# A plan column of the expert stage made 32 bits wide and masked, and one early tile in place of three

## The chip, the cores and the metric

The kernel runs on one core of one Trainium2 chip. The metric is the device time of one execution in microseconds (us). Five engines work side by side, each with an instruction queue of its own: TensorE (PE, matrix products; its weight loads are shown apart as PEld), VectorE (DVE), ScalarE (ACT), GpSimd (POOL) and SyncE (SP), which here only issues transfers (DMA). A name with a q behind it (PEldq, ACTq, SPq) is what the engine's own sequencer does without the engine: loads of registers, sums in registers, issues of transfers. Engines wait for each other through counting semaphores.

## What is computed

4096 tokens of width 256 (64 sequences of 64) go through a conditioned adapter, one attention layer and a mixture of 32 experts, of which each token takes four:

```python
x = adapter(x, cond)                              # down, relu, up, residual
x = x + attention(rmsnorm(x)) @ proj_w            # 16 heads, 64 keys, sinks
h2 = rmsnorm(x)
topv, topi = top_k(h2 @ gate_w + gate_b, 4)
gw = softmax(topv)
for each expert e:                                # W_up 256x512, W_down 256x256
    u, g = split(h2 @ W_up[e])
    y += combine[:, e] * (silu(g) * u @ W_down[e])
out = x_in + x + y
```

Only the experts that a token chose count: 4096 tokens by 4 choices are 16384 pairs of a token and an expert.

## The kernel before

**Two parts.** The first part (adapter, attention, router) ends by writing the chosen rows into lists in memory, one list for each expert (`put`, L673, POOL). The second part, which the change touches, takes the lists in tiles of 128 rows. All values are float32; products are split in two parts, so that an expert's up-product is six matmuls of 512 columns (L971) and its down-product six of 256 (L990).

**The tiles.** How full each list is is known only at run time. The number of tile steps is therefore a fixed upper bound, `NET = PAIRS // P + E - 1 + (AHEAD - 1)`. With `AHEAD = 3` that is 161. For these inputs 142 tiles hold rows; the steps behind them do the same work on rows that go nowhere. The first tiles of the first `AHEAD` experts are at places known beforehand (`begun_slot`, `load_rows` with `i < AHEAD`), and all others come from a plan.

**The plan.** When the router is done, DVE works out the plan (L1559 to L1629) as rows of 256 entries on one partition: `plan_slot` (the offset of the tile's weights in a ring of four experts in SBUF), `plan_wait` (how many experts' weights must have arrived, 1 to 32) and `plan_list` (where the tile's rows lie). The engines read the plan into registers, eight tiles at a time (`BATCH = 8`): PE `plan_slot` (L952) and `plan_wait` (L958), ACT `plan_list` (L1240). `plan_wait` is a tile of type uint16, the other two are int32.

**The loop on PE** (from L1002) does this in step i: the second turn of tile i-2 (`turn_mid`, L980), the first turn of tile i+2 (`turn_in`, L945: two transposes, and the second waits for `s_wready` to reach the register from `plan_wait`), the up-product of tile i (`expert_up`), in every eighth step a read of the plan (`load_slots` at i % 8 == 5, `load_readies` at i % 8 == 6), and the down-product of tile i-3 (`expert_down`).

**Around it.** ACT issues the load of a tile's rows six steps ahead (`load_rows`, L1251), splits, applies silu and scales the result (`rows_out`, L1233). POOL scatters the result rows (L695). SP loads weights (L567) and, once all tiles with rows are through and six more counts of `s_rows_out` have come (`all_out`), starts to read the scattered rows back: eight transfers `picks` of 2 MB (L609) into five buffers; the sixth, seventh and eighth wait until DVE and PE have used a buffer.

**The end.** Behind its last tile, DVE adds up eight groups of picked rows (L1685, L1687, L1690), with no wait but for the picks; PE and ACT add a quarter of each group beside it, the first of them after all scatters have landed; SP and ACT store the result.

Of the kernel before, what the change touches and what calls it, by code (L numbers as in the profile page):

```python
# [8 lines left out]

F32, I32, U32, BF16 = mybir.dt.float32, mybir.dt.int32, mybir.dt.uint32, mybir.dt.bfloat16  # L10
U16 = mybir.dt.uint16
F32R = mybir.dt.float32r
ACT = mybir.ActivationFunctionType
AX = mybir.AxisListType
# [2 lines left out]
P = 128  # L17
# [22 lines left out]
ROW = D + LINE  # L40

PAIRS = NTOK * TOPK
AHEAD = 3
NET = PAIRS // P + E - 1 + (AHEAD - 1)
NET2 = 4 * -(-(NET - P) // 4)
RING = 4
# [18 lines left out]
BATCH = 8  # L65
# [155 lines left out]
def program(nc, d):  # L221
# [4 lines left out]
    def sb(name, shape, dt=F32, stack=ctx):  # L226
        return stack.enter_context(nc.sbuf_tensor(name, shape, dt))
# [19 lines left out]
    expert_no = sb("expert_no", [P, E])  # L247
    begun_slot = sb("begun_slot", [1, AHEAD], I32)

# [115 lines left out]
    plan_f = sb("plan_f", [1, 2 * P])  # L365
    plan_e = sb("plan_e", [1, 2 * P], I32)
    plan_slot = sb("plan_slot", [1, 2 * P], I32)
    plan_wait = sb("plan_wait", [1, 2 * P], U16)
    ring_wait = sb("ring_wait", [1, E], I32)
    all_out = sb("all_out", [1, 1], I32)  # L370
    rows_in = [sb(f"rows_in{i}", [P, ROW]) for i in range(NG)]
# [92 lines left out]
    EARLY, MIDDLE, LATE = 16 * len(early), 16 * len(middle), 16 * len(late)  # L464
    FILL, BEFORE = 16 * (AHEAD + 1), 16 * E
    LAST = NT - 1
# [13 lines left out]
    def sync_program(e):  # L480
# [52 lines left out]
        def load_late():  # L533
            for dst, src in late:
                e.dma_start(dst, src).then_inc(s_late, 16)

            for at in [n * LIST + P for n in range(AHEAD)] + [E * LIST]:
                e.dma_start(lists[at:at + P, :], d["fill_rows"]).then_inc(s_fill, 16)
# [166 lines left out]
    def tensor_program(e):  # L705
# [219 lines left out]
        for h in range(2):  # L925
# [6 lines left out]
        _, at = nc.values_load_multi_w_load_instructions(  # L932
            begun_slot[0:1, 0:AHEAD], engines=[mybir.EngineType.PE], min_val=0, max_val=(RING - 1) * 2 * WE,
            skip_runtime_bounds_check_because="the table holds ring offsets")
        slot_of = {i: (at[i], i + 1) for i in range(AHEAD)}

# [12 lines left out]
        slots, readies = {}, {}  # L949
# [11 lines left out]

        def slot(i):
            if i >= AHEAD:
                slot_of[i] = (slots[i // BATCH][i % BATCH], readies[i // BATCH][i % BATCH])
            return slot_of[i]

        def expert_up(i):
# [34 lines left out]
        for i in range(NET + 3):  # L1002
            if i == 5:
                w.wait_ge(s_plan_list, 1)
            if 2 <= i < NET + 2:
                turn_mid(i - 2)
            if i < NET:
                ready = slot(i)[1]
                if 0 < i < NET - 2:
                    turn_in(i + 2, ready)  # L1010
                else:
                    e.wait_ge(s_wready, ready)
                expert_up(i)
                if i == 0:
                    turn_in(2)

            if i % BATCH == BATCH - 3 and i + 3 < NET:
                load_slots(i // BATCH + 1)
            if i % BATCH == BATCH - 2 and i + 2 < NET:
                load_readies(i // BATCH + 1)  # L1020
            if i >= 3:
                expert_down(i - 3)
# [775 lines left out]
```

## Time and profile before

| | |
|---|---|
| median of 3 runs | 1040.16 us (1039.16 to 1040.64) |
| the profiled execution | 1039.19 us |
| its span, first to last instruction | 1037.4 us |
| the expert stage, from the first tile's up-product to DVE's last tile | 583.1 to 1002.4 us |
| the end, DVE's eight groups and the last store | 1002.4 to 1037.4 us |
| PE busy over the span | 895.6 us (86%) |

The page gives one execution. Read it in three stretches: the first part up to about 556 us, the change-over (plan, last scatters into the lists, first tiles) to about 593 us, and the tiles and the end behind that. The share of PE is a mean over all of them. In the tiles PE goes without a gap, in the change-over it mostly waits. How a stretch ends is read from the chain of work that ended last, and who waited for whom from the idle time that the timeline puts in brackets behind a row.

### The profile page before, as it was taken

The numbers are of one execution on the slowest core, as the hardware profiler recorded it, in microseconds if no ns is written. First come the engines' busy times: TensorE is split into PE (matmuls) and PEld (weight loads), VectorE is DVE, ScalarE is ACT, GpSimd is POOL, SyncE is SP. The second block draws the span as 40 slices with busy tenths as digits, with TensorE's granted clock in tenths as the row PEclk, the third lists the DMA queues.
The fourth block names the chain that finished last, engine by engine and source line by source line (L and its number), as shares of the span: only waits on it lengthen the run. The fifth ranks groups of instructions, "written<-read, shape, count | busy, mean of one in ns | idle before, by whom it ended". The sixth has DMA issues, their size and how long they took to land.

```text
span 1037.4 us, 21388 instructions
## 1 busy us (share of the span) xinstructions
PE 895.6 (86%) x7240; PEld 728.6 (70%) x7272; DVE 804.4 (78%) x1877; ACT 512.5 (49%) x1193; POOL 550.4 (53%) x513
## 2 busy tenths in 40 slices
PE   3859898997899989888851599999999999999985
PEld 2537676675676767567640488888888888888864
DVE  3878799898888889887755377777777777777777
ACT  1223463736445363553751366665665666566631
POOL 2436557877868687887778034333333333333440
PEclk8769999999899999999995699999999999999998
DMA  7235869687796977869875977778677758663589
GB/s 223 61 95 179 267 234 269 212 286 245 243 283 206 291 249 253 271 224 292 306 246 206 336 261 270 277 237 282 238 239 263 257 184 306 227 219 103 189 334 349
DMA packets 127683, 251.93 MB, mean 243 GB/s; under 512 B 18706, under 2 KB 66327, under 8 KB 127002
## 3 DMA queue, kind: packets, MB, share of 16 engines
q1 hardware_dynamic: 83866, 187.59, 54.8%
q0 software_dynamic: 13872, 34.64, 9.2%
q10 hardware_dynamic: 29840, 28.34, 8.8%
q8 instruction: 62, 1.02, 0.4%
q14 instruction: 43, 0.35, 0.1%
HBM read 136.19 MB, written 102.66 MB: 230 GB/s over the span
## 4 chain that ended last, share of the span: by engine, by line
PE 49%; POOL 12%; DMA 12%; DVE 11%; issue 7%; ACT 4%; SPq 4%; ACTq 0%; DVEq 0%; POOLq 0%
PE gbank L971 10%; PE scores L971 10%; POOL lists L673 7%; PE gbank L990 5%; PE scores L990 5%; DMA w_parts<-ring 4%; DMA ring<-in_W_up 3%; PE gbank L762 3%; DMA rows_in<-lists 3%; POOL ring L680 3%; PE gbank L843 3%; PE scores L945 2%; DVE ring L1402 2%; PE gbank L980 2%; PE gbank L945 2%
## 5 line engine op out<-in xcount | busy, mean ns | idle before, releaser
L695 POOL DMA_INDIRECT pick_rows<-rows_out,pair_i x161 | 160.7, 998 | 277.3 <-ACT rows_out L1233 268.5
L680 POOL TENSOR_TENSOR ring<-ring 128x512 fp32r<-128x512 f32 x96 | 123.2, 1296 | 47.3 <-ACT ring L1168 46.6
L971 PE MATMUL scores<-ring,in_part 128*128 x486 | 135.9, 415 | 0.0
L971 PE MATMUL gbank<-ring,in_part 128*128 x480 | 131.8, 409 | 0.0
L673 POOL DMA_INDIRECT lists<-put_rows,slot_i x104 | 101.5, 976 | 49.9 <-issue 27.3
L762 PE MATMUL gbank<-h_t,w_qk 128*128 128x512 f32 x480 | 122.0, 407 | 7.0 <-DVE h_t L1389 4.7
L843 PE MATMUL gbank<-w_o,ring 128*128 128x256 f32 x512 | 118.3, 385 | 3.8 <-ACT ring L1114 3.7
L1402 DVE SCALAR_TENSOR_TENSOR ring<-gbank,b_qk,rope 128x512 f32<-128x512 f32 x160 | 109.9, 744 | 14.7 <-PE gbank L762 14.1
L762 PEld LDWEIGHTS gbank<-h_t,w_qk 128*128 128x128 f32 x480 | 89.6, 191 | 32.2 <-issue 8.6
L843 PEld LDWEIGHTS gbank<-w_o,ring 128*128 128x128 f32 x512 | 96.2, 193 | 17.3 <-ACT ring L1114 5.2
L1168 ACT ACTIVATE ring<-ring 128x512 fp32r<-128x512 f32 x96 | 59.9, 628 | 92.2 <-DMA w_parts<-ring 49.1
L971 PEld LDWEIGHTS scores<-ring,in_part 128*128 128x128 f32 x486 | 86.9, 192 | 15.2
L971 PEld LDWEIGHTS gbank<-ring,in_part 128*128 128x128 f32 x480 | 84.3, 189 | 14.5
L990 PEld LDWEIGHTS gbank<-ring,mid_part 128*128 128x128 f32 x486 | 67.1, 188 | 14.6 <-issue 8.1
L1219 ACT ACTIVATE in_part<-scores,norm_w 128x128 fp32r<-128x128 f32 x162 | 50.8, 365 | 51.8 <-PE scores L945 33.4
L990 PE MATMUL gbank<-ring,mid_part 128*128 x486 | 70.3, 280 | 4.2 <-issue 4.1
L990 PEld LDWEIGHTS scores<-ring,mid_part 128*128 128x128 f32 x480 | 66.8, 188 | 7.2
L990 PE MATMUL scores<-ring,mid_part 128*128 x480 | 68.2, 278 | 0.0
L1649 DVE SCALAR_TENSOR_TENSOR mid<-scores,rows_in,silu 128x256 f32<-128x256 f32 x81 | 39.1, 483 | 36.7 <-ACT silu L1225 36.7
L1225 ACT ACTIVATE silu<-scores,rows_in 128x256 f32<-128x256 f32 x81 | 38.6, 477 | 52.0 <-PE scores L971 51.9
L1639 DVE TENSOR_TENSOR pair_i<-rows_in,twice 128x1 int32<-128x1 f32 x161 | 25.7, 160 | 49.0 <-ACT in_part L1219 40.0
L1649 DVE SCALAR_TENSOR_TENSOR mid<-gbank,rows_in,silu 128x256 f32<-128x256 f32 x80 | 38.5, 482 | 27.1 <-ACT silu L1225 27.1
(200 smaller groups left out, 1879.2 us busy)
## 6 DMA issues: line engine op xcount, KB each, us to landing
w_parts<-ring SPq DMA_DIRECT2D x192, 256.0 KB, 3.3
ring<-w_parts SPq DMA_DIRECT2D x32, 1536.0 KB, 7.6
rows_in<-lists ACTq DMA_DIRECT2D x161, 136.0 KB, 4.0
ring<-in_W_up SPq DMA_DIRECT2D x64, 256.0 KB, 3.5
picks<-pick_rows SPq DMA_DIRECT2D x8, 2048.0 KB, 11.9
ring<-in_W_down SPq DMA_DIRECT2D x32, 256.0 KB, 4.0
q_r<-rot SPq DMA_DIRECT2D x16, 512.0 KB, 6.8
q_r<-ring SPq DMA_DIRECT2D x16, 512.0 KB, 6.5
```

The costliest lines, as they stand in the source:

```text
L673: e.indirect_dma_start(out=lists, out_offset=bass.IndirectOffsetOnAxis(ap=slot_i[r % NPAY][:, s * TOPK + k:s * TOPK + k + 1], axis=0), in_ ...
L680: e.tensor_tensor(lower, lower.bitcast(F32), upper.bitcast(F32), ALU.subtract).then_inc(s_lower, 1)
L695: e.indirect_dma_start(out=pick_rows, out_offset=bass.IndirectOffsetOnAxis(ap=pair_i[:, i:i + 1], axis=0), in_=rows_out[i % NY][:, :], in_ ...
L762: ins = e.matmul(bank[:, :], w_qk[:, x, c, 2 * j + o, :], h_t[i][:, y, c, :], start=k == 0, stop=k == len(CHUNK_PRODUCTS) - 1)
L843: ins = e.matmul(bank[:, 0:D], y_t[:, n // REP, n % REP, :, :].rearrange("p b s -> p (b s)"), w_o[:, n, :], start=False, stop=n == 2 * REP ...
L945: ins = e.transpose(bank[:, c * P:(c + 1) * P], rows_in[i % NG][:, c * P:(c + 1) * P], ident[:, :])
L971: ins = e.matmul(front[i % FRONTS], in_parts[i % IN_BUFS][x][:, c, :], ring[:, bass.ds(at + y * WE + c * 2 * DFF, 2 * DFF)], start=k == 0, ...
L990: ins = e.matmul(out, mid_parts[i % 2][x][:, c, :], ring[:, bass.ds(at + y * WE + KC * 2 * DFF + c * D, D)], start=k == 0, stop=k == len(C ...
L1168: e.activation(w_upper[q % NU], w_third[q % NW].bitcast(F32), ACT.Copy).then_inc(s_upper, 1)
L1219: ins = e.activation(in_parts[i % IN_BUFS][0][:, c, :], front[i % FRONTS][:, c * P:(c + 1) * P], ACT.Copy, scale=norm2_w[:, c:c + 1])
L1402: e.scalar_tensor_tensor(out=by_seq(t[n][:, :]), in0=by_seq(gbank[banks[o]][:, :]), scalar=b_qk[:, 2 * j + o:2 * j + o + 1], in1=rope[:, t ...
L1649: e.scalar_tensor_tensor(out=mid[i % MID_BUFS][:, :], in0=front[i % FRONTS][:, 0:DFF], scalar=rows_in[i % NG][:, D + 2:D + 3], in1=silu[i ...
```

## The change

Three things are edited. `AHEAD` goes from 3 to 1: only the first tile of the first expert is begun without the plan, the second and third tile come from the plan as well, the bound `NET` falls from 161 to 159, and with it the steps of PE, DVE, ACT and POOL; `begun_slot`, the rows of `list_begin` and `tile_no` and the number of lists that are filled beforehand follow. `plan_wait` becomes int32. And the value that `turn_in` waits for is masked with 63 in a register. The tiles that hold rows are 142 as before.

```diff
-U16 = mybir.dt.uint16
...
-AHEAD = 3
+AHEAD = 1
 NET = PAIRS // P + E - 1 + (AHEAD - 1)
...
-    plan_wait = sb("plan_wait", [1, 2 * P], U16)
+    plan_wait = sb("plan_wait", [1, 2 * P], I32)
...
             if i >= AHEAD:
-                slot_of[i] = (slots[i // BATCH][i % BATCH], readies[i // BATCH][i % BATCH])
+                slot_of[i] = (slots[i // BATCH][i % BATCH], readies[i // BATCH][i % BATCH] & 63)
             return slot_of[i]
```

On PE, this is the step in which `plan_wait` is read for the second time (i = 6), before the change: the second turn of one tile and the first turn of another (both transposes in one row, x2), the up-product, the read.

```order
478 L980 MATMUL gbank<-ident,mid 128x128 x2
479 L945 MATMUL scores<-ident,rows_in 128x128 x2
480 L971 ISA
481 L971 MATMUL gbank<-ring,in_part 128x512
482 L971 ISA
483 L971 MATMUL gbank<-ring,in_part 128x512 x2
484 L971 ISA
485 L971 MATMUL gbank<-ring,in_part 128x512
486 L971 ISA
487 L971 MATMUL gbank<-ring,in_part 128x512 x2
488 L958 TENSOR_LOAD plan_wait
489 L990 ISA
```

The same step on PE after the change (line numbers are one lower, since a line of the file is gone; an ISA row is a sum in registers that makes an address):

```order
488 L979 MATMUL gbank<-ident,mid 128x128 x2
489 L944 MATMUL scores<-ident,rows_in 128x128
490 L943 REGISTER_ALU
491 L944 MATMUL scores<-ident,rows_in 128x128
492 L970 ISA
493 L970 MATMUL gbank<-ring,in_part 128x512
494 L970 ISA
495 L970 MATMUL gbank<-ring,in_part 128x512 x2
496 L970 ISA
497 L970 MATMUL gbank<-ring,in_part 128x512
498 L970 ISA
499 L970 MATMUL gbank<-ring,in_part 128x512 x2
500 L957 TENSOR_LOAD plan_wait
```

One register operation has come between the two transposes of `turn_in`, in this step and in every other one that takes its wait from the plan (158 tiles). Nothing else on PE moved; the 21st reads of `plan_slot` and `plan_wait`, for tile 160, are gone with the last two steps.

On ACT, this is the start of the row loads before the change, three of them ahead of the read of the plan:

```order
408 L1251 DMA rows_in<-lists 128x272 x3
409 L1240 TENSOR_LOAD plan_list
410 L1251 REGISTER_ALU
411 L1251 DMA rows_in<-lists 128x272
412 L1251 REGISTER_ALU
```

And after it:

```order
408 L1250 DMA rows_in<-lists 128x272
409 L1239 TENSOR_LOAD plan_list
410 L1250 REGISTER_ALU
411 L1250 DMA rows_in<-lists 128x272
412 L1250 REGISTER_ALU
413 L1250 DMA rows_in<-lists 128x272
```

The read of the plan has moved ahead of the loads of tiles 1 and 2, and each of these two takes a register operation of its own. DVE, POOL and SP keep their order; DVE and POOL do two tiles fewer at the end, and SP fills two lists fewer at the start of the program.

## Rows read from the trace of the kernel before

**Rows 1.** Timeline of PE: start, us, engine line; the up-products of tiles 8 and 48.
```profile
606.24 1.65 PE L971 MATMUL scores<-ring,in_part 128*128 x6
...
707.42 1.64 PE L971 MATMUL scores<-ring,in_part 128*128 x6
```

**Rows 2.** Lines L958, L952: ns min/median/max, first and last start; last row 605 to 710.
```profile
L958 PEldq TENSOR_LOAD <-plan_wait x21: 1923/2011/2420, 563.8 to 992.6; - x21
...
L952 PEldq TENSOR_LOAD <-plan_slot x21: 587/594/1532, 562.2 to 988.5; - x21
...
L958 PEldq TENSOR_LOAD <-plan_wait x5: 1927/1977/2042, 619.9 to 700.9; - x5
```

**Rows 3.** Line L958 from 743 to 746 us, and PE's timeline there (tile 62).
```profile
L958 PEldq TENSOR_LOAD <-plan_wait x1: 1923/1923/1923, 743.6 to 743.6; - x1
...
745.05 1.65 PE L971 MATMUL gbank<-ring,in_part 128*128 x6
```

**Rows 4.** The same around tile 54: weight loads and PE; idle time before in brackets.
```profile
723.29 0.20 PEld L945 LDWEIGHTS scores<-ident,rows_in 128*128 128x128 f32 x2 [0.38 <-DMA rows_in<-lists]
...
L958 PEldq TENSOR_LOAD <-plan_wait x1: 2072/2072/2072, 723.9 to 723.9; - x1
...
726.15 0.98 PE L990 MATMUL gbank<-ring,mid_part 128*128 x6 [1.02 <-issue]
```

**Rows 5.** PEld's waits, 593 to 988.9 us (total, times, longest); PE's timeline, tiles 3, 157.
```profile
PEld gbank L990 <- issue: 6.5, 8, 1.4
PEld scores L945 <- DMA rows_in<-lists: 1.1, 3, 0.5
...
593.02 1.18 PE L971 MATMUL gbank<-ring,in_part 128*128 x4
...
988.90 1.65 PE L971 MATMUL scores<-ring,in_part 128*128 x6
```

**Rows 6.** Register operations of L971 (PE) and L1251 (ACT); L945's transposes: busy, mean ns.
```profile
L971 PEldq FUSED_REGOPS  x644: 42/46/51, 582.9 to 996.7; - x161
...
L1251 ACTq ALU_OP  x158: 46/46/53, 575.8 to 984.3; - x158
...
L945 PE MATMUL gbank<-ident,rows_in 128*128 128x128 f32 x160 | 31.1, 277 | 1.1 <-DMA rows_in<-lists 1.1
```

**Rows 7.** The chain that ended last, 555 to 600 us: start, us, what.
```profile
569.60 3.84 DMA lists<-q_r,slot_i
...
575.07 0.74 ACTq L1240
...
575.99 11.49 DMA rows_in<-lists
...
587.52 0.69 PE gbank L945 x2
```

**Rows 8.** PE's timeline over the last tiles; first row and last from the chain.
```profile
984.41 7.57 DMA rows_in<-lists
...
992.22 1.65 PE L971 MATMUL gbank<-ring,in_part 128*128 x6
994.70 0.97 PE L990 MATMUL gbank<-ring,mid_part 128*128 x6 [0.82 <-issue]
...
995.64 1.65 PE L971 MATMUL gbank<-ring,in_part 128*128 x6
...
1002.37 1.68 DVE picks L1685
```

**Rows 9.** SP's timeline; stretches: busy by engine, PE clock, DMA share, GB/s; the chain's end.
```profile
974.07 44.50 SPq L609 DMA_DIRECT2D picks<-pick_rows  x8
...
1000.00:1005.00 5.00, 4.87 (x33) 4.30 (x32) 4.69 (x7) 2.03 (x5) 3.26 (x3) 1.00 0.78 299
1005.00:1010.00 5.00, 2.80 (x13) 2.11 (x12) 4.90 (x6) 0.00 (x0) 3.05 (x2) 1.00 0.56 177
...
1030.64 0.96 DVE resid L1690
```

## The prediction

> **What bounds the kernel now.** I read the timeline of PE over the tiles first, then the registers' reads, then the change-over and the end.
>
> In the tiles PE's array is the bound. The up-product of tile 8 starts at 606.24 us and that of tile 48 at 707.42 [rows 1]: 40 steps in 101.18 us, 2.53 us each. A step has no idle time of PE in it; what the array has to do more adds to the time, and what lies in PE's sequencer alone adds nothing as long as the sequencer is ahead of the array.
>
> That it is ahead can be seen. In these 101 us PE's sequencer read `plan_wait` five times, and each read held it for 1.93 to 2.04 us [rows 2]; the step stayed 2.53. At tile 62 the read starts at 743.6 although it is queued behind the up-product that the array begins only at 745.05 [rows 3]: a lead of 1.45 us, to which the 1.65 us of that up-product is added. A read of 1.92 us is over at 745.5, before the array runs dry.
>
> Where the lead is lost, the read shows. At tile 54 a late load of rows held PE for 0.38 us, the read began at 723.9, behind the start of its own tile's up-product (723.29 plus 0.20, 723.5), took 2.07 us, and the down-product began only at 726.15 with 1.02 us of idle time put down to "issue" [rows 4]. The waits of the weight loads list eight such places between 593 and 988.9 us, all of them in one form, the one behind `plan_wait` [rows 5]. `plan_slot`, as many entries of 32 bits, takes 0.594 us in the middle, against 2.011 [rows 2].
>
> In the change-over the chain runs through the last scatters into the lists, then ACT's load of tile 3, 11.49 us under way, then PE [rows 7]. At the end it runs through DVE's eight groups, 1002.37 to 1031.60 us without a gap [rows 8, 9], with the picks' transfers beside it.
>
> **The change part by part.** All sums are made against the profiled execution, 1039.19 us (span 1037.4).
>
> *The 32-bit read, 21 times, then 20.* From tile 3 (593.02) to tile 157 (988.90) there are 154 steps in 395.88 us [rows 5]. At 2.53 (101.18/40) they would take 389.54; 6.34 are stalls. 1.1 of it are three waits for rows [rows 5]; the other 5.2 are the eight reads. (The row's own 6.5 counts from the idle weight loader and is an upper end.) If the new read costs what `plan_slot` costs, the worst case of tile 54 reads: 723.9 plus 0.59 is 724.5, while the array is on the up-product until 723.5 plus 1.65, 725.1. Nothing is left. Gain 5.2; with the three waits for rows it could at most be 6.3. A read that is only a little shorter gains less; that is the first rival. The first read, before tile 0, is hidden by the wait for rows either way. DVE writes one row of 256 entries as 32 bits in place of 16, before the same wait.
>
> *Two steps fewer.* The 142 tiles with rows are the same in both kernels, so the picks start behind the same tile. What goes are two of the steps behind them: 2 times 2.53, 5.06 us, on PE, which is on the path until DVE's first group.
>
> *The last tiles' stalls.* From tile 157 to 158 the step is 3.32 (988.90 to 992.22), to 159 it is 3.42 [rows 5, 8]. The first is the wait for the last rows: their load was issued at 984.41, ten microseconds behind the first picks (974.07), and took 7.57 us [rows 8, 9]. The last load of the new kernel is issued two steps earlier behind the picks, so it still arrives in time. The second is the 21st read of `plan_wait`, which is gone [rows 8]. 0.79 and 0.89, together 1.7.
>
> *The register operation, 158 times.* The trace of before has none like it on PE. The nearest rows: 644 fused sums of registers on the same sequencer at 46 ns behind L971 alone, and ACT's single sum at 46 ns [rows 6]. Below end: 0, hidden by the lead. Upper end: 158 times 0.046, 7.3 us. I take 0, since in [rows 1, 2] the sequencer gets back 2.0 plus 0.6 us of reads in eight steps without a stall, at least 0.32 a step, which is seven times the new operation; and the reads then want 1.2 in place of 2.6.
>
> *The start.* Tile 0's rows are loaded as before. Tiles 1 and 2 now come behind the read of the plan (0.74 us [rows 7]); the plan is long there, since the loads wait for the last scatters. PE turns tile 3 before the second up-product, and tile 3's load has the same transfers and the same read ahead of it, plus two register operations and moves, about 0.1 each. Loss 0.25; upper end 1.0, if tile 1's late load binds. The weights of experts 1 and 2 are wanted later than before, which costs nothing.
>
> *The end.* DVE's groups start 5.06 plus 1.7, 6.8 us nearer to the first picks. Does the transfer hide that? Between 974.07 and the end the DMA engines are filled but for 1000 to 1010 us, where the shares are 0.78 and 0.56 [rows 9]: 5 times 0.22 plus 5 times 0.44, 3.3 us free. Two row loads of 136 KB less at about 0.3 MB a us give 0.9. If all of that traffic has to be moved, the end can come only 4.2 us nearer to the first picks, and 2.6 are given back. If the later transfers, which wait for buffers, have slack, nothing is. The first five are under way at once, so they land before they are wanted; the sixth to eighth wait for buffers and stay close to DVE. I take the middle, 1.3.
>
> Sum: 5.2 + 5.06 + 1.7 - 0.25 - 1.3 = 10.4 us, 1028.8 for an execution like the profiled one. That one is at the low end of the three runs, 0.97 below their median; I add half of it: **1029.3 us**.
>
> **The rivals.**
>
> *The read stays long.* The column is read at another place than `plan_slot`; if it is the place or the time and not the 16 bits that makes 2.0 us, little is gained. With none of the 5.2 us won the time is 1034.5. For it: 2.011 us are 251 ns for each of eight registers, which looks like one trip after another. Against it: eight registers of 32 bits take 74 ns each, on the same engine, one step earlier [rows 2]. The Trainium skill (Runtime: NRT & Kernel Launch, Instruction fetch mechanics) puts a register's load at about 200 ns even in bulk; by that rule a read of eight would take 1.6 us whatever its width, an estimate, eight stalls would lose at most 8 times 0.41, 3.3 us, and the time would be 1031.2 or more. The trace disagrees with it for 32 bits and comes near it for 16.
>
> *The transfers bind the end.* The full 2.6 us are given back: 1030.6.
>
> *The register operation shows.* If the sequencer has no time to spare, 7.3 us come back (158 times 46 ns): 1036.6, still 0.3% faster. Against it stand the steps of 2.53 with two reads in every eight.
>
> *Slower.* The wait of the second transpose takes its value from a register that has just been written. If PE's sequencer ran the operation only when the first transpose has left the array, the lead would be gone in each tile, and a step would grow by up to one transpose, 277 ns [rows 6]: 158 times 0.277 is 43.8, that is 1029.3 + 43.8 = 1073.1 us. It decides from 66 ns a tile (10.4/158). Against it: the fused sums stand between matmuls too, and their products' addresses come from them at once, with no gap.
>
> **How the numbers follow.** The forecast 0.73; the transfers bind the end 0.12; the read stays long 0.05; the register operation shows 0.06; slower 0.04. Range: the best sum is 6.3 + 5.06 + 1.7 with nothing given back, 13.1, which is 1026.1; the worst within the forecast gives back 2.6 and loses 1.0 at the start, 8.4, which is 1030.8, or 1031.8 with the whole distance to the median; the first rival takes it to 1034.5. 1026 to 1034.5 leaves out the register cases and the tails, under 0.2. What this kernel's measurement can tell from no change is about 0.2%, 2.1 us: faster 0.92, within it 0.04 (the register operation together with the transfers, 1038), slower 0.04.
>
> **What the profile of the changed kernel would show.** The reads of `plan_wait` at about 0.6 us, 20 of them; no "issue" idle time ahead of L990 in the gbank form; steps of 2.53 throughout, so that tile 3 to tile 157 take about 390.6; the last L971 row followed by DVE's first group without a wait for rows; picks starting about 5 us earlier, DVE's first group about 12. A step of 2.57 to 2.58 would mean that the register operation shows; idle time ahead of L945's second transpose, that the lead is lost; a gap between DVE's groups or PE waiting for picks longer than now, that the transfers bind. The prediction is wrong if the reads are not shorter or the step grows.

## The result, and the profile after the change

The changed kernel takes **1031.08 us** (median; the kernel before, timed beside it, 1040.52), a ratio of **0.9914 with a 95% interval of 0.9889 to 0.9938**: between 6.5 and 11.5 us faster. The forecast was 1029.3 us in a range of 1026 to 1034.5, 10.9 us faster. A second comparison of the same two kernels gave 1034.03 against 1041.13, 0.9918 (0.9897 to 0.9939). (The ratios are taken over all the runs, not from the two medians.) The time lies in the range both times. The accounts below show that the size came out nearly right partly by terms that cancel.

The profiled execution of the changed kernel took 1029.53 us, its span is 1027.7 (before: 1039.19 and 1037.4). Its line numbers are one lower than those of before: L958 is now L957, L971 is L970, L990 is L989, L1685 is L1684.

The reads of the registers and the new operation, in the changed kernel (ns minimum/median/maximum, first and last start in us):

```profile
L957 PEldq TENSOR_LOAD <-plan_wait x20: 587/590/692, 563.7 to 965.9; - x20
...
L951 PEldq TENSOR_LOAD <-plan_slot x20: 587/592/1584, 562.0 to 963.3; - x20
...
L943 PEldq ALU_OP  x156: 32/32/42, 587.1 to 981.9; - x156
```

The read of `plan_wait` fell from a median of 2.011 us [rows 2] to 0.590, that is what `plan_slot` takes. The mask is there as a 32 ns operation of PE's sequencer, 156 times between two transposes. (The section on the change said 158: the other two masks belong to the last two steps, which have no first turn left, and stand ahead of the up-product.) The waits of the weight loads from 590 to 1000 us (total, times, longest), first in the kernel before, then in the changed one; [rows 5] has the stretch from 593 to 988.9 us alone:

```profile
PEld gbank L990 <- issue: 7.8, 9, 1.4
PEld scores L945 <- DMA rows_in<-lists: 1.9, 4, 0.8
```

```profile
PEld gbank L944 <- DMA rows_in<-lists: 1.9, 2, 1.2
PEld scores L944 <- DMA rows_in<-lists: 0.5, 1, 0.5
PEld scores L989 <- issue: 0.4, 1, 0.4
```

The "issue" time behind the reads is gone, 6.5 us between tiles 3 and 157 and 7.8 up to 1000 us; the one of 0.4 is in the other form. Waits for rows are 2.4 us, all of them between tile 3 and the fourth last, where they were 1.1 in that stretch. Now PE's timeline, the up-products of tiles 3, 32, 48, 155 and 158 (start, us):

```profile
590.94 1.40 PE L970 MATMUL gbank<-ring,in_part 128*128 x5
...
665.92 1.64 PE L970 MATMUL scores<-ring,in_part 128*128 x6
...
706.62 1.64 PE L970 MATMUL scores<-ring,in_part 128*128 x6
...
980.10 1.63 PE L970 MATMUL gbank<-ring,in_part 128*128 x6
...
987.28 1.64 PE L970 MATMUL gbank<-ring,in_part 128*128 x6
```

This is the surprise. From tile 32 to 48 the 16 steps take 40.70 us, **2.544 us each and not 2.53**. Nothing waits there; the step itself is longer. The products behind it, first in the kernel before, then in the changed one (640 to 960 us: busy us, mean ns of one, idle before):

```profile
L990 PE MATMUL gbank<-ring,mid_part 128*128 x372 | 53.6, 280 | 3.0 <-issue 3.0
L990 PE MATMUL scores<-ring,mid_part 128*128 x372 | 52.8, 277 | 0.0
```

```profile
L989 PE MATMUL gbank<-ring,mid_part 128*128 x378 | 55.2, 282 | 0.0
L989 PE MATMUL scores<-ring,mid_part 128*128 x375 | 54.8, 282 | 0.0
```

At the end, DVE's eight groups (first and last start) and, in the changed kernel, the one wait among them:

```profile
L1685 DVE TENSOR_TENSOR picks<-picks x8: 1748/1750/1753, 1002.3 to 1027.9; 128x1536 f32<-128x1536 f32 x8
```

```profile
L1684 DVE TENSOR_TENSOR picks<-picks x8: 1749/1751/1758, 991.6 to 1018.3; 128x1536 f32<-128x1536 f32 x8
...
  DMA picks<-pick_rows: 1.0, 1
```

The two profiles differ by 9.7 us of span. Put together from the starts of the up-products and of DVE's groups:

| stretch | before, us | after, us | difference |
|---|---|---|---|
| up to tile 0's up-product | 583.13 | 582.92 | -0.2 |
| tile 0 to tile 3 | 9.89 | 8.02 | -1.9 |
| tile 3 to the fourth last tile (157, now 155) | 395.88 | 389.16 | -6.7 |
| from there to DVE's first group | 13.4 | 11.5 | -1.9 |
| DVE's first group to its last | 25.6 | 26.7 | +1.1 |
| from there to the end | 9.5 | 9.4 | -0.1 |

The -6.7 of the third row are four things: two steps fewer, -5.06; 152 steps that are each 13.9 ns longer (means of the undisturbed steps 2.5432 and 2.5293), +2.1; the reads' stalls gone, -5.26; and 1.5 us more of waiting for rows.

### The profile page after: what moved, and what is told of

The parts are those of the page before. It is cut to its first block, busy times and chain, and to the rows that moved or that the text cites. A ratio compares the mean times of both kernels' runs of the same rounds, so it can differ in the third digit from the quotient of the medians.

```text
span 1027.7 us, 21467 instructions
## 1 busy us (share of the span) xinstructions
PE 891.4 (87%) x7240; PEld 727.2 (71%) x7240; DVE 802.3 (78%) x1865; ACT 509.0 (50%) x1185; POOL 549.9 (54%) x511
## 4 chain that ended last, share of the span: by engine, by line
PE 48%; POOL 14%; DMA 13%; DVE 9%; issue 8%; SPq 5%; ACT 3%; ACTq 0%; POOLq 0%; DVEq 0%
PE scores L970 10%; PE gbank L970 10%; POOL lists L672 9%; PE scores L989 5%; PE gbank L989 5%; DMA w_parts<-ring 4%; PE gbank L761 4%; DMA rows_in<-lists 3%; DMA ring<-in_W_up 3%; POOL ring L679 3%; PE gbank L842 3%; PE gbank L944 2%; DVE ring L1401 2%; PE gbank L979 2%; PE scores L944 2%
## 5 line engine op out<-in xcount | busy, mean ns | idle before, releaser
L970 PE MATMUL scores<-ring,in_part 128*128 x480 | 132.2, 411 | 0.0
L970 PE MATMUL gbank<-ring,in_part 128*128 x474 | 129.3, 408 | 0.0
L970 PEld LDWEIGHTS scores<-ring,in_part 128*128 128x128 f32 x480 | 85.1, 191 | 14.3
L970 PEld LDWEIGHTS gbank<-ring,in_part 128*128 128x128 f32 x474 | 83.2, 189 | 13.8
L989 PEld LDWEIGHTS scores<-ring,mid_part 128*128 128x128 f32 x480 | 68.0, 190 | 7.4 <-issue 0.4
L989 PEld LDWEIGHTS gbank<-ring,mid_part 128*128 128x128 f32 x474 | 67.2, 190 | 6.9
L989 PE MATMUL scores<-ring,mid_part 128*128 x480 | 70.2, 283 | 0.1
L989 PE MATMUL gbank<-ring,mid_part 128*128 x474 | 69.3, 282 | 0.0
L1648 DVE SCALAR_TENSOR_TENSOR mid<-gbank,rows_in,silu 128x256 f32<-128x256 f32 x79 | 38.1, 482 | 26.9 <-ACT silu L1224 26.9
```

The lines of the kernel that those rows point to most:

```text
L970: ins = e.matmul(front[i % FRONTS], in_parts[i % IN_BUFS][x][:, c, :], ring[:, bass.ds(at + y * WE + c * 2 * DFF, 2 * DFF)], start=k == 0, ...
L989: ins = e.matmul(out, mid_parts[i % 2][x][:, c, :], ring[:, bass.ds(at + y * WE + KC * 2 * DFF + c * D, D)], start=k == 0, stop=k == len(C ...
L1648: e.scalar_tensor_tensor(out=mid[i % MID_BUFS][:, :], in0=front[i % FRONTS][:, 0:DFF], scalar=rows_in[i % NG][:, D + 2:D + 3], in1=silu[i ...
```

## The experiments

The table collects what the sections below read from the profiles: the step (mean of the steps under 2.6 us between tile 3 and the fourth last), what the other steps take above it, tile 0 to tile 3, and the address of `mid_part00` modulo 256 bytes, from the program's layout. Ratios are each against the kernel before timed beside it.

| kernel | ratio (95% interval) | step, us | excess, us | tile 0 to 3, us | address mod 256 |
|---|---|---|---|---|---|
| before | 1 | 2.529 | 6.4 | 9.89 | 192 |
| changed | 0.9914 (0.9889 to 0.9938) | 2.543 | 2.6 | 8.02 | 128 |
| e1, begin only | 0.9964 (0.9938 to 0.9990) | 2.543 | 6.8 | 7.90 | 128 |
| e2, mask only | 0.9979 (0.9954 to 1.0003) | 2.530 | 6.5 | 8.30 | 192 |
| e3, 32 bits and mask | 0.9944 (0.9921 to 0.9967) | 2.530 | 4.3 | 8.18 | 192 |
| e4, longer column only | 0.9996 (0.9970 to 1.0023) | 2.530 | 5.7 | 10.11 | 192 |
| e5, changed, all up 64 bytes | 0.9924 (0.9898 to 0.9950) | 2.530 | 4.8 | 8.21 | 192 |
| e6, before, all up 64 bytes | 1.0043 (1.0013 to 1.0073) | 2.552 | 5.8 | 7.89 | 0 |
| e7, changed, `mid_parts` up 64 | one run, 1028.85 us | 2.531 | 1.6 | 7.79 | 192 |
| e8, changed again | 0.9918 (0.9897 to 0.9939) | 2.543 | 1.5 | 7.86 | 128 |
| e9, as e7 | 0.9905 (0.9873 to 0.9938) | 2.531 | 4.6 | 7.86 | 192 |
| e10, ten tiles fewer | 0.9888 (0.9863 to 0.9913) | 2.543 | 2.4 | 8.29 | 128 |

### The parts one at a time

The theory on record was: the 32-bit read takes the stalls away, the mask costs nothing, two steps are worth their 5 us less what the end gives back. The longer step had been seen by then, and the expectations of e2 and e3 put it down to the mask. Four kernels, made from the kernel before: the short begin, the mask, the 32 bits with the mask, and a control.

**e1, the shorter begin alone.**

```diff
-AHEAD = 3
+AHEAD = 1
```

> One early tile in place of three, alone: the plan's waits stay 16 bits wide and unmasked. Theory (the read's width and the two steps are separate gains): reads of the waits still 2.0 us, about eight stalls of 5 us in sum between tile 3 and tile 155, step 2.53 us, but the last steps without their two stalls, so about 6.8 us nearer at the end less 1.0 given back there: about 1034.5 us. Rival (the early tiles matter at the start as well): 2 us less, 1032.5.

Measured: 1036.56 us, 0.9964. The reads, and the waits of the weight loads from 590 to 1000 us:

```profile
L958 PEldq TENSOR_LOAD <-plan_wait x20: 1927/2028/2289, 566.6 to 973.2; - x20
```

```profile
PEld gbank L990 <- issue: 4.5, 5, 1.2
PEld scores L945 <- DMA rows_in<-lists: 2.4, 2, 1.6
PEld gbank L945 <- DMA rows_in<-lists: 1.5, 2, 1.1
```

The 16-bit reads are as long as before and still stall: with one of 0.4 us in the other form, 4.9 us at six places. The time is 2 us above the 1034.5 expected, which had steps of 2.53, for the begin alone also brings the longer step: from tile 16 to tile 31 the up-products start at

```profile
627.82 1.64 PE L971 MATMUL scores<-ring,in_part 128*128 x6
...
665.97 1.64 PE L971 MATMUL gbank<-ring,in_part 128*128 x6
```

that is 38.15 us for 15 steps, 2.543 each, in a kernel that has no mask. So the mask is not what makes the step longer.

**e2, the mask alone.**

```diff
-                slot_of[i] = (slots[i // BATCH][i % BATCH], readies[i // BATCH][i % BATCH])
+                slot_of[i] = (slots[i // BATCH][i % BATCH], readies[i // BATCH][i % BATCH] & 63)
```

> The mask alone: 16-bit waits, three early tiles, 161 tiles. Theory (the register operation is what lengthens the step by 14 ns): step 2.544 us, 158 times 14 ns are 2.2 us more, and the stalls behind the 2 us reads at least as long as before, 5 to 8 us: 1042.5 to 1046 us. Rival (the step grew because everything behind the wider row lies 512 bytes further in SBUF): step 2.53, 1040.5 us.

Measured: 1038.69 us, 0.9979, not to be told from no change; the 1042.5 to 1046 us of the expectation did not come. The operation is there, the step is 2.530, and the stalls behind the reads are too:

```profile
L944 PEldq ALU_OP  x156: 32/32/42, 586.0 to 984.7; - x156
```

```profile
PEld gbank L990 <- issue: 7.1, 8, 1.3
```

156 times 32 ns would be 5.0 us; 155 steps at 2.530 in place of 2.529 are 0.1. The mask is hidden.

**e3, the wide column with the mask, begin unchanged.** The diff is e2's and this line:

```diff
-    plan_wait = sb("plan_wait", [1, 2 * P], U16)
+    plan_wait = sb("plan_wait", [1, 2 * P], I32)
```

> 32-bit waits with the mask, but three early tiles and 161 tiles. Theory: reads 0.59 us, no stall behind them (5.2 and 0.9 us gone), step 2.544 (2.2 us more): about 1036.5 us. Rival (the early tiles cause the stalls behind the reads, not their width): stalls stay, 1042 us.

Measured: 1033.75 us beside 1040.73 for before, 7.0 less; 0.9944. That is 2.8 below the 1036.5 expected, which had the longer step. The reads, the waits that are left, and DVE's groups:

```profile
L958 PEldq TENSOR_LOAD <-plan_wait x21: 587/592/762, 562.5 to 986.9; - x21
```

```profile
PEld scores L945 <- DMA rows_in<-lists: 3.4, 4, 2.0
PEld gbank L945 <- DMA rows_in<-lists: 0.8, 1, 0.8
PEld gbank L990 <- issue: 0.4, 1, 0.4
```

```profile
L1685 DVE TENSOR_TENSOR picks<-picks x8: 1748/1751/1758, 995.9 to 1021.7; 128x1536 f32<-128x1536 f32 x8
```

Of "issue" 0.4 us are left, as in the changed kernel. The fourth last tile is 11.5 us ahead of DVE's first group instead of 13.4, so the last tiles' stalls went with the reads. DVE's groups span 25.8 us, as before: with the old number of steps nothing is given back at the end.

**e4, the column longer, not wider.** Widening the column also moves every buffer behind it by 512 bytes. This does that alone, with 16 bits.

```diff
-    plan_wait = sb("plan_wait", [1, 2 * P], U16)
+    plan_wait = sb("plan_wait", [1, 4 * P], U16)
...
-        e.tensor_scalar(plan_wait[:, :], plan_row, 1.0, None, ALU.add).then_inc(s_plan, 1)
+        e.tensor_scalar(plan_wait[:, 0:2 * P], plan_row, 1.0, None, ALU.add).then_inc(s_plan, 1)
```

> The row of waits is given 512 more bytes that nothing uses, so that all behind it lies where it does with 32-bit waits; nothing else is changed. Theory: step 2.53, 1040.5 us. Rival (the layout lengthens the step): step 2.544, 1042.7 us.

Measured: 1041.3 us, 0.9996. Reads of

```profile
L958 PEldq TENSOR_LOAD <-plan_wait x21: 1925/1962/2335, 566.7 to 995.7; - x21
```

and a step of 2.530. So it is the width that shortens the read: in e3 the column lies at the same address as before, and a shift by 512 bytes of what lies behind it does nothing. (The width and the distance between two entries were changed together, and the 32-bit column without the mask was not tried.)

### Where the longer step comes from

What e1 changes besides the order is the size of two tables: `pair_i` and `twice` have one column for each tile, 159 in place of 161, and every buffer behind them lies 64 bytes lower. Against this theory (the addresses) stands the rival that the order of the begin itself does it.

**e5, the changed kernel with the old addresses modulo 256.**

```diff
-    pair_i = sb("pair_i", [P, NET], I32)
-    twice = sb("twice", [P, NET])
+    pair_i = sb("pair_i", [P, NET + 2], I32)
+    twice = sb("twice", [P, NET + 2])
```

> The whole change, but pair_i and twice keep their 161 columns, so that rows_in and all buffers behind it lie 64 bytes higher, at the same address modulo 128 as in the kernel before. Theory (the addresses make the step 14 ns longer, not the shorter begin): the down-product back at 278 to 280 ns a matmul, a step of 2.53 us, 156 steps 2.2 us shorter than in the changed kernel; if the picks' transfers hold the end as in the changed kernel, up to half of it is given back, so 1028.8 to 1030 us. Rival (it is the shorter begin itself): 282 to 284 ns, a step of 2.544 us, and 1031 us as in the changed kernel.

**e6, the kernel before, its buffers 64 bytes higher.**

```diff
+    line_pad = sb("line_pad", [P, 16])
     rows_in = [sb(f"rows_in{i}", [P, ROW]) for i in range(NG)]
```

> The kernel before with 64 bytes of padding ahead of rows_in, so that the buffers behind it lie at 0 modulo 128 as in the changed kernel; nothing else. Theory of the addresses: the down-product at 282 to 284 ns, a step of 2.544 us, 155 steps 2.2 us longer: 1042.7 us, ratio 1.002. Rival (the shorter begin): a step of 2.53 us and no difference. For the start: if the clock's rise after the first tile comes about 8 us after its up-product, as in the kernel before, or about 4 us, as in the changed kernel, it tells whether that difference between two profiles belongs to the change.

**e7, the changed kernel, with `mid_parts` moved by 64 bytes and what lies behind it by 128.** Ahead of it nothing moves. (Of the expectation's "modulo 128" only that much holds: modulo 256 the buffers behind are moved as well.)

```diff
+    pad_front = sb("pad_front", [P, 16])
     mid_parts = [[sb(f"mid_part{i}{h}", [P, FC, P], F32R) for h in range(2)] for i in range(2)]
+    pad_back = sb("pad_back", [P, 16])
     resid = sb("resid", [P, NT, D])
```

> The whole change with 64 bytes of padding ahead of mid_parts and 64 behind: mid_parts alone lies at 64 modulo 128, all else at 0 modulo 128 as in the changed kernel. If the stationary operand of the down-product is what the address slows: 278 to 280 ns a matmul and a step of 2.53 us. If it is another buffer (in_parts, mid, silu, rows_out): 282 to 284 ns and 2.544 us.

Measured. In e5 the 16 steps from tile 26 to 42 begin and end at

```profile
653.23 1.65 PE L970 MATMUL gbank<-ring,in_part 128*128 x6
...
693.70 1.65 PE L970 MATMUL gbank<-ring,in_part 128*128 x6
```

40.47 us, 2.529 each: with the old addresses the step is the old one, although the begin is the short one. In e6 the 16 steps from tile 24 to 40 are

```profile
646.67 1.65 PE L972 MATMUL scores<-ring,in_part 128*128 x6
...
687.47 1.64 PE L972 MATMUL scores<-ring,in_part 128*128 x6
```

40.80 us, 2.550 each, with the old begin and neither read nor mask changed; the whole kernel is slower than before, 1.0043 (1.0013 to 1.0073). The rival falls: **the addresses lengthen the step**, by 14 ns in the changed kernel and by 22 in e6. The theory was too coarse in one thing, e6 is further off than the 14 ns that equal places modulo 128 would give: modulo 256 the three positions that occurred go with 2.53 (192), 2.543 (128) and 2.552 (0). That the pattern repeats is shown for 512 bytes alone (e4); a shift by 256 was not tried.

e7 brings the step to 2.531, 12 of the 13.9 ns, by moving `mid_parts` and what lies behind it. `rows_in`, `in_parts`, `silu` and `mid` lie where the changed kernel has them. The down-products of e7 did not fall to the 278 to 280 ns that were expected, though; in e9, the same kernel (640 to 960 us):

```profile
L991 PE MATMUL gbank<-ring,mid_part 128*128 x378 | 54.7, 280 | 0.0
L991 PE MATMUL scores<-ring,mid_part 128*128 x374 | 54.3, 281 | 0.0
```

The ends of matmuls are modelled in these records, the starts are not. So the step is cut here at the starts of its parts (us, means over the 142 to 148 steps under 2.6 us of each profile):

| kernel | up-product to down-product | down-product to the turns | turns to the next up-product |
|---|---|---|---|
| before | 1.485 | 0.690 | 0.355 |
| e5 | 1.486 | 0.689 | 0.355 |
| changed | 1.475 | 0.713 | 0.356 |
| e6 | 1.481 | 0.716 | 0.355 |
| e7 | 1.469 | 0.707 | 0.355 |
| e9 | 1.470 | 0.706 | 0.355 |

In the changed kernel the down-product takes 23 ns more and the up-product 10 less. e5 puts both back, but e7 and e9 do not: the down-product gets back 6 or 7 of the 23 ns, and the other 5 or 6 of the 12 come off the up-product, although `in_parts`, which it reads, has not moved. So e7's step has the length of the old one without being the old one, and that the position of `mid_parts` alone slows the down-product is not shown. Which buffers count, and why a position costs time, stays open.

### What it is worth, and the end

**e8, the changed kernel once more**, timed beside e9 and e10.

> The changed kernel once more, beside the two below. For its size: 1031 us and a ratio of 0.991. For the waits for rows at tiles 4 to 55, which were 1.1 to 4.9 us in the profiles so far: theory (transfers of rows and weights that meet in one order or another) they differ again from the 2.6 us of its first profile; rival (a cost of the change) they stay within 0.3 us of it.

Measured: 1034.03 us, 0.9918. Its ratio is that of the first comparison; its 1034.03 is 3 us above the 1031 expected, while the kernel before came out only 0.6 higher beside it. The waits for rows are not a cost of the change:

```profile
PEld gbank L944 <- DMA rows_in<-lists: 1.9, 2, 1.1
PEld scores L944 <- DMA rows_in<-lists: 0.4, 2, 0.3
```

These sum to 2.3 here and 2.4 in the first profile, but what they add to the steps is 1.5 against 2.6 us, and over all kernels the waits from 590 to 1000 us run from 1.4 (e2) to 4.5 (e5) without order: with long reads 1.9, 1.4, 3.9, 4.2 and 2.1 (before, e2, e1, e4, e6), with short ones 2.4, 4.2, 4.5, 1.5, 2.3, 4.4 and 2.4 (changed, e3, e5, e7 to e10).

**e9, e7 with an interval.**

> The whole change with mid_parts alone at 64 modulo 128, the kernel whose one run took 1028.85 us, now with its interval. Theory (the step is 2.53 us and what it saves is kept but for half): 1 to 2 us below the changed kernel beside it. Rival (waits for rows take it up, as with all buffers shifted): the same as the changed kernel.

Measured: 1030.15 us, 0.9905 (0.9873 to 0.9938); e8 beside it 1034.03, 0.9918 (0.9897 to 0.9939). The step is 2.531, but its profile lost 4.6 us in excess against 1.5. The two intervals overlap nearly whole. e5, whose step is as short, had 0.9924 (1033.03 us, 3 above the 1030 that was the most expected of it). That the 2 us of step are saved shows in the profiles; that the kernel is faster by them isn't shown by these runs.

**e10, ten steps fewer.** 149 tiles are enough for these inputs, of which 142 have rows; for another routing they would not be, so this is a probe of the end and no kernel to use.

```diff
-NET = PAIRS // P + E - 1 + (AHEAD - 1)
+NET = PAIRS // P + E - 1 + (AHEAD - 1) - 10
...
-    pair_i = sb("pair_i", [P, NET], I32)
-    twice = sb("twice", [P, NET])
+    pair_i = sb("pair_i", [P, NET + 10], I32)
+    twice = sb("twice", [P, NET + 10])
```

> The whole change with ten more tile steps left out: 149, which hold all the rows of these inputs (142 tiles have any), so the output is the same for these inputs, though not for every routing; the buffers lie where the changed kernel has them. It shows how far steps at the end are worth their time. If steps off the end are given back once the picks' transfers bind: the transfers run at 394 to 399 GB/s from 975 to 1005 us; ten tiles' rows are 1.4 MB less, 3.5 us, and what else the end gives is VectorE's start, 9.5 us (the picks' landing) behind 970 us, so 1022 to 1027 us. If nothing is given back: ten steps of 2.54 us, 1006 us.

Measured: 1029.92 us, 0.9888, 4.1 below e8. From tile 0's up-product to the end it took 440.46 us where the two profiles of the changed kernel took 444.78 and 443.86. So 25.4 us of steps gave 3.4 to 4.3 us. The theory's 3.5 us for the rows that are not loaded fit that; its 1022 to 1027 was counted from 1031 and is missed by 3, as e8 is. DVE's waits from 975 us to the end, and two stretches (busy us by PE, PEld, DVE, ACT, POOL, then the granted clock, the DMA share and GB/s), in e10:

```profile
DVE picks L1684 <- DMA picks<-pick_rows: 21.7, 8, 9.0
```

```profile
985.00:990.00 5.00, 2.83 (x7) 2.30 (x8) 3.28 (x4) 0.00 (x0) 0.00 (x0) 0.66 1.04 416
990.00:995.00 5.00, 1.98 (x7) 1.35 (x6) 1.92 (x2) 0.39 (x1) 0.00 (x0) 0.84 1.02 408
```

DVE, which in the changed kernel works 4.9 of 5 us in its groups (995 to 1015 us), now waits for each of its eight groups, 21.7 us in all, and the DMA engines are full. Past the changed kernel, transfers set the end.

## Why the prediction was right

**The read, 5.2 us.** Right in mechanism and size. 5.26 us of stalls went, and e3 shows it without the shorter begin and at the same place. The rival "the read stays long" is dead. The forecast showed at one place, tile 54, that a late load of rows takes the sequencer's lead; the trace of before shows it at all eight. By its semaphore records the rows that PE's sequencer waits for in the step of the read landed 0.2 to 1.8 us before the up-product where the read stalled, and 2.6 to 4.9 us before it at the eleven reads that did not. At six of the eight no idle time of PE tells of it beforehand. The rival's estimate rests on the Trainium skill (Runtime: NRT & Kernel Launch, Instruction fetch mechanics), which puts a register's load at about 200 ns even in bulk. For the 32-bit column that does not hold here: eight registers in 590 ns are 74 each. For 16 bits, 2.0 us for eight, 251 each, it is near. (The page speaks of register loads that the runtime adds, not of a column in SBUF.)

**Two steps, 5.06 us.** Right: tile 155 stands where 157 stood.

**The last tiles' stalls, 1.7 us.** 13.4 to 11.5, 1.9 us. Right in size. In e3, which has the old number of steps, both stalls are gone too (11.5 us), so the last rows' lateness need not come from the number of steps, as the forecast had it. Of the five profiles with 161 steps three have a longer step there (3.32 in before, 3.35 in e4, 2.85 in e6) and two have not (2.53 in e2 and e3); of the six with 159 none has. The wait came and went at the same number of steps, and the kernel before was profiled with it.

**The mask, nothing.** Right: e2's step is 2.530 with it. The two that counted on it, 1036.6 and 1073.1, are excluded.

**The start, a loss of 0.25 us.** Not resolved. The stretch from tile 0 to 3 got 1.9 us shorter, but that need not be the change. The granted clock is back at 2.4 GHz (1.00) in the changed kernel at 588, about 5 us after tile 0's up-product; in the kernel before it is still at 1.2 (0.50) there. The rows are the same stretch, before and after, then e6 at the same distance from its tile 0 (584.92):

```profile
588.00:589.00 1.00, 1.00 (x5) 0.50 0.19 66
```

```profile
588.00:589.00 1.00, 1.00 (x7) 1.00 0.06 19
```

```profile
590.00:591.00 1.00, 1.00 (x9) 1.00 0.21 70
```

(Columns: the stretch, its length, PE's busy time and operations, the granted clock, the DMA share, GB/s.) e6 has nothing of the change and rises early. Of the twelve profiles ten need 7.8 to 8.3 us from tile 0 to 3, and before and e4, which stay longer at the lower level, 9.9 and 10.1. In the ten the level rises 2.9 to 3.9 us after tile 0's up-product, in the two after 7.9 and 8.8. Both late ones begin three tiles early, but so do e2, e3 and e6, which rise early. Among the ten the stretch takes 7.9 to 8.3 us with three early tiles and 7.8 to 8.3 with one, so a loss of 0.25 can't be seen. Whether the timed executions of the kernel before rise early or late isn't seen either.

**The end, 1.3 us given back.** Right in size, though 1.3 was only the middle between nothing and 2.6. The picks start 3.8 us earlier than before (974.07 [rows 9]; the forecast said about 5):

```profile
970.27 37.03 SPq L608 DMA_DIRECT2D picks<-pick_rows  x8
```

DVE's first group starts 10.7 us earlier (about 12 in the forecast), so it is 6.9 us nearer to the first picks, where the forecast had 6.8. DVE's groups span 26.7 and 26.9 us in the two profiles of the changed kernel, against 25.6 before and 25.8 in e3, 0.9 to 1.3 more. The place, in the chain that ended last in the changed kernel:

```profile
996.52 5.80 DMA pick_rows<-rows_out,pair_i
...
1002.46 0.39 ACT resid L1286
...
1006.94 11.35 DMA picks<-pick_rows
...
1018.31 1.77 DVE picks L1684
```

The eighth group waits 1.0 us for its picks. The rival's 2.6 didn't come, but the gap that the forecast saw between 1000 and 1010 us [rows 9], shares of 0.78 and 0.56, is used up:

```profile
1000.00:1005.00 5.00, 2.10 (x5) 1.75 (x6) 4.90 (x5) 0.77 (x2) 0.00 (x0) 0.50 1.03 399
1005.00:1010.00 5.00, 5.00 (x22) 4.27 (x22) 4.90 (x6) 0.77 (x2) 0.00 (x0) 0.90 1.04 413
```

**What was missing: the step.** "Steps of 2.53 throughout" and 390.6 us from tile 3 to 157 failed. The step is 2.543, 2.1 us over 152 steps, by a cause that stood in no part of the sum: a size in a table's declaration moved buffers by 64 bytes. The forecast's last line calls it wrong "if the reads are not shorter or the step grows", and the step did grow: in that sign it was wrong, for it knew one cause of a longer step, the mask, and left out the layout. The sign that I had set for the mask, 2.57 to 2.58, would have been misread had it been nearer; only e1 and e2 apart told the two from each other.

The account without the start: 5.26 + 5.06 + 1.9 - 2.1 - 1.5 - 1.1 + 0.1 = 7.6 us in the profiles; the two comparisons gave 9.4 and 7.1 by their medians, 8.9 and 8.5 by their ratios. The forecast's 10.4 lacks the 2.1 of the step; the 1.5 us of rows are in this one pair of profiles and not the change's. That the two profiles differ by 9.7 us, so near to the 10.4 of the sum, is luck: the start's 1.9 us, which no part of the change was shown to bring, made up for most of the step's 2.1. With the step's 2.1 us in the sum the forecast would have been 1031.4.

## What to carry to other kernels

A register read from a table costs by the entry's width, here 2.0 us for eight entries of 16 bits and 0.6 for eight of 32. It is hidden as long as the sequencer is ahead, and shows where a load that came late, even without holding up the matmuls, has just cost the lead. When a change resizes any table, compare the addresses behind it before and after, and pad the table to its old size if a single part is to be measured. Steps taken from the tail of a loop are worth their time only until the transfers that follow have no free time left; here that point is reached.

## What the runs showed of the hardware that was not expected

- Eight registers took 0.59 to 0.76 us from a 32-bit column (medians 590 and 592 ns) and 1.92 to 2.42 us from a 16-bit one, on the same engine at the same place in the program (changed, e3, against before, e1, e4). The width is not the whole rule: PE's single read of `begun_slot`, 32 bits too, took 1.12 us for three registers (before) and 0.66 for one (changed). Why, stays open.
- A tile of the same instructions took 2.53, 2.543 or 2.552 us by the position of its buffers alone, 192, 128 or 0 modulo 256 bytes for `mid_part00` (e5 and e6 against their counterparts). Only these three were seen, and which buffers count is not settled.
- The granted clock came back to 1.00 early in the first tiles in ten profiles and late in two (before and e4), which is worth 1.9 us in a profile. No part of the change was shown to go with it.
